# Inverse deviations of all norms: GpSimd's power instruction in place of a guess and three Newton steps on VectorE

## The reference

```
layernorm(x) = (x - mean) / sqrt(var + 1e-5)          over the 512 features of a token
layer 0: autocorrelation attention, 8 bit linear layer
layer 1: grouped attention (32 heads, 8 kv heads, biased), gated experts of rank 16
layer 2: group-wise multiplicative attention, whose result passes a group norm
         (y - mu) * rsqrt(var + 1e-5) over 16 channels x 512,
         then a permuted block-diagonal ffn with GELU
layer 3: grouped attention with rotary positions and a causal mask, SwiGLU ffn with NF4 weights
```

## Time and profile before

| | |
|---|---|
| median of 3 runs | 2106.98 us (2104.03 to 2108.8) |
| the profiled execution | 2104.66 us |
| its span in the trace | 2102.5 us |
| instructions in the trace | 26370 |
| mean granted clock of TensorE | 0.919 of full speed |
| busy, PE / PEld / DVE / ACT / POOL | 1799.7 / 1465.7 / 1516.9 / 1070.9 / 1038.0 us |

### The profile page before, as it was taken

How to read it: one execution, slowest core, us unless ns; L and a number is a source line. 1 busy time by engine, 2 the same in 40 slices (tenths; PEclk the granted TensorE clock), 3 DMA queues, 4 the chain that set the end, 5 groups by cost and what they waited for, 6 DMA issues and landing times.

```text
span 2102.5 us, 26370 instructions
## 1 busy us (share of the span) xinstructions
PE 1799.7 (86%) x8645; PEld 1465.7 (70%) x8645; DVE 1516.9 (72%) x2735; ACT 1070.9 (51%) x2556; POOL 1038.0 (49%) x889
## 2 busy tenths in 40 slices
PE   5665689999999999757677689999999999778879
PEld 3444477788888888645454478888888888657757
DVE  6666589999999985468543678888888888747740
ACT  2432467877877875431233255555555643335630
POOL 3555265555555555432133166776776742016620
PEclk7887799999999999878777899999999999889989
DMA  3002011111112111210001111111111110111120
GB/s 115 6 1 77 26 57 50 46 56 61 46 56 61 46 51 31 66 43 1 0 1 60 36 39 48 36 46 41 36 51 36 36 51 1 42 30 51 38 69 35
DMA packets 54135, 88.06 MB, mean 42 GB/s; under 512 B 9008, under 2 KB 15792, under 8 KB 53744
## 3 DMA queue, kind: packets, MB, share of 16 engines
q1 hardware_dynamic: 54000, 86.39, 13.1%
HBM read 75.62 MB, written 10.75 MB: 41 GB/s over the span
## 4 chain that ended last, share of the span: by engine, by line
PE 25%; DVE 22%; issue 19%; POOLq 13%; POOL 8%; ACT 7%; DVEq 5%; DMA 1%; SPq 0%; ACTq 0%
POOLq L326 8%; DVE b_st_u L253 6%; POOLq L324 5%; PE c_ps L66 4%; PE a_ps L66 4%; PE e_ps L66 3%; DVEq L254 3%; PE b_ps_o L66 3%; POOL d_roped L1026 3%; PE d_ps_job L66 2%; PE b_ps_job L66 2%; PE d_ps_o L66 2%; ACT b_st_sign L234 1%; POOL d_wo L1031 1%; POOL d_pt_sign L323 1%
## 5 line engine op out<-in xcount | busy, mean ns | idle before, releaser
L66 PE MATMUL b_ps_o<-b_wo,b_oT 128*128 128x512 f32 x768 | 190.0, 397 | 18.1 <-DVE b_oT L1273 18.1
L66 PE MATMUL d_ps_o<-d_wo,d_oT 128*128 128x512 f32 x768 | 190.7, 397 | 9.9 <-DVE d_oT L1272 9.7
L1026 POOL TENSOR_TENSOR d_roped<-d_rot_a,d_rot_b 128x512 f32<-128x512 f32 x80 | 104.6, 1307 | 183.6 <-DVE d_rot_b L1282 183.6
L66 PE MATMUL d_ps_job<-xnT,d_wq 128*128 128x512 f32 x768 | 193.1, 404 | 2.3 <-DVE d_rot_b L1282 2.3
L66 PE MATMUL b_ps_job<-xnT,b_wq 128*128 128x512 f32 x768 | 189.5, 400 | 5.0 <-DVE b_qT L1273 4.9
L323 POOL TENSOR_SCALAR b_pt_sign<-b_pt_sign 128x512 f32<-128x512 f32 x112 | 79.5, 710 | 222.0 <-ACT b_pt_sign L315 211.6
L66 PEld LDWEIGHTS b_ps_o<-b_wo,b_oT 128*128 128x128 f32 x768 | 145.2, 191 | 54.4 <-DVE b_oT L1273 24.4
L253 DVE SCALAR_TENSOR_TENSOR b_st_u<-b_st_sign,b_st_u 128x512 f32<-128x512 bf16 x182 | 176.2, 968 | 9.1 <-issue 0.4
L66 PEld LDWEIGHTS d_ps_o<-d_wo,d_oT 128*128 128x128 f32 x768 | 143.2, 188 | 47.7 <-DVE d_oT L1272 15.5
L66 PEld LDWEIGHTS b_ps_job<-xnT,b_wq 128*128 128x128 f32 x768 | 142.7, 191 | 35.7 <-issue 7.1
L66 PEld LDWEIGHTS d_ps_job<-xnT,d_wq 128*128 128x128 f32 x768 | 143.1, 191 | 33.5 <-issue 3.3
(11 more groups left out here) (366 smaller groups left out, 4453.8 us busy)
## 6 DMA issues: line engine op xcount, KB each, us to landing
b_raw<-in_wq_dram SPq DMA_DIRECT2D x32, 256.0 KB, 2.6
b_raw<-in_wo_dram SPq DMA_DIRECT2D x32, 256.0 KB, 2.6
d_raw<-in_wq_dram SPq DMA_DIRECT2D x32, 256.0 KB, 2.6
d_raw<-in_wo_dram SPq DMA_DIRECT2D x32, 256.0 KB, 2.7
e_nat<-dequantized SPq DMA_DIRECT2D x30, 256.0 KB, 2.9
b_st_v<-in_quantized_dram SPq DMA_DIRECT2D x13, 256.0 KB, 2.9
dequantized<-b_st_u SPq DMA_DIRECT2D x13, 256.0 KB, 2.8
a_ctx_in<-in_ctx_dram SPq DMA_DIRECT2D x8, 256.0 KB, 5.3
```

The costliest lines, as they stand in the source:

```text
L66: i = pe.matmul(out, a, b, start=first and t == 0, stop=last and t == len(terms) - 1)
L1026: pool.tensor_tensor(roped[:, n % 2], rot_a[:], rot_b[:], ALU.add).then_inc(s_sum, 1)
```

## The change

`inverse_root` goes. VectorE ends a norm with `bn_aggr` and signals `means`. GpSimd then adds epsilon, drains, and raises the result to the power of a tile that holds -0.5 (`root`), and signals; in stage `a` GpSimd makes the shift too. In stages `c` and `e` VectorE waits for the root at a later due time, so that other work of its plan may stand in between. For the group norm VectorE still adds epsilon and GpSimd does the power alone. To free semaphores, `s_early` is merged into `s_wide` (5 transfers in place of 2 and 3), `s_rows` into `s_const` (9 in place of 4 and 5), and the two `rates` semaphores of stage `a` into one. The place of each new piece in GpSimd's and VectorE's order is in the yields. The core of the diff:

```diff
-def inverse_root(dve, y, v, t, iterations=3):
-    dve.tensor_scalar(y.bitcast(I32), v.bitcast(I32), -0.5, float(0x5F3759DF), ALU.mult, ALU.add)
-    dve.drain()
-    for _ in range(iterations):
-        dve.tensor_tensor(t, y, y, ALU.mult)
-        dve.drain()
-        dve.scalar_tensor_tensor(t, t, -0.5, v, ALU.mult, ALU.mult)
-        dve.drain()
-        dve.scalar_tensor_tensor(y, t, 1.5, y, ALU.add, ALU.mult)
-        dve.drain()
...
 class QuadNorm:
-    def rates_of_stats(self, dve):
+    def means(self, dve):
         for j in range(QUAD):
-            dve.bn_aggr(self.mv[:, j], self.stats[:, j])
-        dve.drain()
-        dve.tensor_scalar(self.var[:], self.mv[:, :, 1], EPS, None, ALU.add)
-        dve.drain()
-        inverse_root(dve, self.rstd[:], self.var[:], self.tmp[:])
+            i = dve.bn_aggr(self.mv[:, j], self.stats[:, j])
+        return i
+
+    def root(self, pool):
+        pool.tensor_scalar(self.var[:], self.mv[:, :, 1], EPS, None, ALU.add)
+        pool.drain()
+        return pool.tensor_tensor(self.rstd[:], self.var[:], self.power[:], ALU.pow)
...
         # stage a, GpSimd
+            def quad(t):
+                n = norm[t]
+                yield 0.0
+                pool.memset(n.power[:], -0.5)
+                for k, name in enumerate(("rates1", "rates2", "rates3")):
+                    yield at(QUAD * t, name) + 0.1
+                    pool.wait_ge(s_means, 2 * k + t + 1)
+                    pool.tensor_scalar(shift[t][:], n.mv[:, :, 0], -1.0, None, ALU.mult)
+                    n.root(pool)
+                    pool.drain()
+                    pool.tensor_tensor(shift[t][:], shift[t][:], n.rstd[:], ALU.mult).then_inc(s_rates, 1)
...
         # stage c, GpSimd
+                def root(step, k):
+                    yield at(t, step) + 1.0
+                    waits(pool, t, ("dve", "means", k))
+                    done(norm[t].root(pool), ("root", k))
+
                 for j in J:
                     yield at(t, "cs", j)
...
+                if t:
+                    yield at(t, "rates")
+                    before(pool, 4)
+                    pool.memset(norm[t].power[:], -0.5)
+                yield from root("rates", 0)
                 for j in J:
                     yield at(t, "ffn") - 0.5
...
+                yield from root("norm2", 1)
...
+                yield at(t, "grp") + 1.0
+                waits(pool, t, ("dve", "gvar", 0))
+                done(pool.tensor_tensor(grstd[t][:], gvar[t][:], norm[t].power[:], ALU.pow), ("groot", 0))
+                yield from root("norm3", 2)
                 for h in H:
                     yield at(t, "up", h + 1)
...
+                yield from root("norm4", 3)
...
         # stage c, VectorE
+                def rates(step, k):
+                    norm[t].statistics(dve, x[t])
+                    done(norm[t].means(dve), ("means", k))
+                    yield at(t, step) + 2.5
+                    waits(dve, t, ("pool", "root", k))
...
-                norm[t].rates(dve, x[t])
+                yield from rates("norm2", 1)
...
-                inverse_root(dve, grstd[t][:], gvar[t][:], gtmp[t][:])
+                yield at(t, "grp") + 2.0
+                waits(dve, t, ("pool", "groot", 0))
...
         # stage e, GpSimd and VectorE
+            for half in (0, 1):
+                yield (0.5, 9.0)[half]
...
+                pool.wait_ge(s_means, half + 1)
+                norm[half].root(pool).then_inc(s_root, 1)
...
-                    norm[half].rates(dve, [resid[:, HALF * half + j] for j in range(HALF)])
+                    norm[half].statistics(dve, [resid[:, HALF * half + j] for j in range(HALF)])
+                    norm[half].means(dve).then_inc(s_means, 1)
+                    yield (2.0, 10.0)[half]
+                    dve.wait_ge(s_root, half + 1)
```

More of the change, by code:

```diff
@@ L339, in __init__, with statistics @@
         self.mv = sb(name + "_mean_var", [P, QUAD, 2])
-        self.var, self.rstd, self.tmp = (sb(name + x, [P, QUAD]) for x in ("_var", "_rstd", "_tmp"))
-    def rates(self, dve, xs):
+        self.var, self.rstd, self.power = (sb(name + x, [P, QUAD]) for x in ("_var", "_rstd", "_power"))
+    def statistics(self, dve, xs):
         for j in range(QUAD):
@@ L530, in chain @@
                 done(pool.tensor_tensor(x(b), x(b), bias8[:], ALU.add), "x1b")
-            yield from in_order(*(chain(b) for b in B))
+            def quad(t):
[9 more added lines that the diff above has]
+                    pool.tensor_tensor(shift[t][:], shift[t][:], n.rstd[:], ALU.mult).then_inc(s_rates, 1)
+            yield from in_order(*(quad(t) for t in (0, 1)), *(chain(b) for b in B))
         def tensor(pe):
@@ L711, in quad, with means @@
                 n = norm[t]
[L713 to L716, removed]
+                def means():
+                    n.means(dve).then_inc(s_means, 1)
                 yield at(QUAD * t, "rates1")
@@ L727, in quad @@
                     dve.drain()
-                    rates()
+                    means()
             def chain(b):
@@ L1463, in expert_group_and_permuted_ffn @@
         hT = [a[:, :, 0].rearrange("p a (j n) -> p a j n", j=QUAD) for a in xp]
-        s_small, s_early, s_wide, s_wb, s_down, s_rows, s_const = (sem(n) for n in ("small", "early", "wide", "wb_in", "down_in", "rows", "const"))
+        s_small, s_wide, s_wb, s_down, s_const = (sem(n) for n in ("small", "wide", "wb_in", "down_in", "const"))
         s_zero, s_wm, s_high, s_split, s_pick = (sem(n) for n in ("zero", "product", "high", "split", "pick"))
@@ L1488, in expert_group_and_permuted_ffn @@
         turned_order = lambda n, m: [(n, 0), (n, 1), (n, 2), (m, 0), (n, 3), (m, 1), (m, 2), (m, 3)]
[L1489 to L1492, removed]
+        dve_s = [Steps(sem(f"dve{t}"), of("y") + [("means", 0), ("xn1", 0), ("xn1", 1)] + turned_order("xn1", "t1")[2:] + [("z", 0), ("hw", 0), ("hT", 0)]
+                       + of("x1") + [("means", 1)] + of("xn2", "p") + [("row", 0), ("grp", 0), ("gvar", 0), ("affine", 0)]
+                       + of("x2") + [("means", 2)] + turned_order("xn3", "t3") + of("pick", "yT", "x3") + [("means", 3)] + turned_order("xn4", "t4")) for t in (0, 1)]
+        pool_s = [Steps(sem(f"pool{t}"), of("cs") + [("root", 0)] + of("xb") + [("root", 1)] + [(n, j) for j in J for n in ("xs", "xc")]
+                        + [("groot", 0), ("root", 2)] + [("acts", h) for h in H] + [("root", 3)]) for t in (0, 1)]
         steps = {"pe": pe_s, "act": act_s, "dve": dve_s, "pool": pool_s}
@@ L1550, in gpsimd @@
             pool.memset(raw[:, 2], 0.0).then_inc(s_zero, 1)
+            pool.memset(norm[0].power[:], -0.5)
             def thread(t):
                 done = pool_s[t].done
+                def root(step, k):
+                    yield at(t, step) + 1.0
+                    waits(pool, t, ("dve", "means", k))
+                    done(norm[t].root(pool), ("root", k))
                 for j in J:
@@ L1825, in thread @@
                 before(dve, 4 if t else 2)
-                norm[t].rates(dve, x[t])
+                yield from rates("rates", 0)
                 for j in (0, 1):
@@ L1903, in thread @@
                 dve.drain()
-                dve.tensor_scalar(gvar[t][:], gvar[t][:], EPS, None, ALU.add)
-                dve.drain()
-                inverse_root(dve, grstd[t][:], gvar[t][:], gtmp[t][:])
+                done(dve.tensor_scalar(gvar[t][:], gvar[t][:], EPS, None, ALU.add), ("gvar", 0))
+                yield at(t, "grp") + 2.0
+                waits(dve, t, ("pool", "groot", 0))
                 dve.tensor_tensor(g_a[t][:], grp[t][:, :, 0], grstd[t][:], ALU.mult)
@@ L1919, in thread @@
                 dve.drain()
-                norm[t].rates(dve, x[t])
+                yield from rates("norm3", 2)
                 yield from turned("xn3", "t3", 0)
@@ L1935, in thread @@
                 dve.drain()
-                norm[t].rates(dve, x[t])
+                yield from rates("norm4", 3)
                 yield from turned("xn4", "t4", 0)
@@ L2001, in swiglu @@
         s_down, s_x, s_out = sem("down"), sem("x"), sem("out")
+        s_means, s_root = sem("means"), sem("root")
         TILE = 12 * 3.0
@@ L2067, in gpsimd @@
         def gpsimd(pool):
-            yield 0
+            for half in (0, 1):
+                yield (0.5, 9.0)[half]
+                if half == 0:
+                    before(pool, 4)
+                    for t in (0, 1):
+                        pool.memset(norm[t].power[:], -0.5)
+                pool.wait_ge(s_means, half + 1)
+                norm[half].root(pool).then_inc(s_root, 1)
             for n in range(pt.total):
```

48 lines of the change are left out of this document (13 added, 35 removed).

## The result

| | kernel before | changed kernel |
|---|---|---|
| median of the timed executions | 2105.51 us (4) | 2071.27 us (4) |
| profiled execution / its span | 2104.66 / 2102.5 | 2073.24 / 2071.5 |
| mean granted clock of TensorE | 0.919 | 0.931 |
| VectorE busy | 1516.9 us | 1474.0 us |
| GpSimd busy | 1038.0 us | 1065.6 us |

The ratio is 0.9844 (95% interval 0.9801 to 0.9887). In a second comparison it is 0.9857 (0.9826 to 0.9887), with a median of 2070.31. So the change gains 30 to 35 us: 33 and 30 by the two ratios, 34 and 35 by the medians, 31 between the two profiled executions. 28 were forecast, and 2079 us. One execution of the kernel before took 6034.96 us and is left out everywhere. VectorE's busy time falls by 42.9 us, more than the 31 named as the least.

What follows compares the result with a forecast made beforehand. Attention stages were taken as TensorE-bound, the short stages as chains of hand-overs with no engine full. Eight terms summed to 27.7, say 28 us, off the profiled 2104.7: 2076.7, as a median 2079; range 2066 to 2108.

Steps and rivals of the forecast that it cites:

- 1, start: Start of the first layer: first root 0.8 us quicker, query product taken by VectorE at 19.7 instead of 21.8; 2.1 us gained.
- 2, its last sequence: First layer's last sequence: VectorE's low half, which TensorE waits for, no longer stands behind a whole iteration; 2.7 us gained.
- 3, second and third norm: First layer, 205 to 221 us: the two roots end at 208.2 and 212.7, the second instead of 220.8; 7 us counted.
- 4, its tail: Tail of the first attention: VectorE makes a late unit's probabilities right after the aggregation, 6.3 us sooner; 5.0 us counted.
- 5, expert layer, first half: First half of the tokens: quicker roots, gate arithmetic free of bias additions, low half before the wait; 8 us counted.
- 6, second half: Expert layer, second half: one root gains 1.2 us, roots queued behind GpSimd's low halves lose 5.8; net -4.6.
- 7, norm 4: Fourth norm of the expert layer: 3.3 us gained in the first half, 1.2 in the second; 4.5 together.
- 8, last layer: Last layer: first norm 0.3 us, second 2.7 as TensorE's low half now precedes the wait; 3.0 together.
- The price: Time of one GpSimd power instruction, at every root: at least 0.2 us, at most 3.4, taken as 1.0.
- The slope: Ten of the places go with the power's price one to one: gain is 28 - 10 (p - 1) us.
- the dear cases: Rivals at the roots: power 2 to 3.6 us, gains 2 to 18, chance 0.13; from 4.2 us slower, chance 0.17.
- The rival of the factor 1.9: Every root 1.9 times as long on GpSimd, power 4.6 us, 2115 us in all; within the slower case, chance 0.17.

Runs made afterwards that it cites:

- again: The changed kernel run once more, unaltered, for a closer ratio and a second trace; median 2070.31 us, ratio 0.9857.
- the order alone: Changed kernel's order of work, but guess and Newton steps back on VectorE and no root on GpSimd; 2105.54 us, ratio 1.0026 to the kernel before.
- the engine alone: Changed kernel, but in expert and last layers VectorE waits for each root directly behind its aggregation; 2080.57 us, ratio 0.9902 to the kernel before.
- the third trace of before: The kernel before, unaltered, traced a third time; 2097.20 us, one execution.

## Why the prediction was right

| step | forecast | changed | again |
|---|---|---|---|
| 1, start | 2.1 | 3.3 | 3.6 |
| steady part of the first layer | - | 7.3 | 12.1 |
| 2, its last sequence (180 to 190) | 2.7 | 3.4 | 3.3 |
| 3, second and third norm (190 to 242) | 7 | 7.6 | 7.8 |
| first attention | - | -2.9 | -2.9 |
| 4, its tail (895 to 947) | 5.0 | 4.8 | 4.7 |
| 5, expert layer, first half (to 1010) | 8 | 7.9 | 7.9 |
| 6, second half (to 1113) | -4.6 | -5.2 | -5.1 |
| 7, norm 4 (to 1187) | 4.5 | 2.5 | 2.4 |
| second attention | - | -1.7 | -1.7 |
| 8, last layer | 3.0 | 3.9 | 3.8 |
| sum | 27.7 | 30.9 | 35.9 |

The eight steps alone give 28.2 us in the first trace. What the forecast lacked is two things that half cancel: the steady part, and 4.6 us that the two attention stages give back. That the eight steps add up so near to 27.7 is in part luck: in the first trace steps 1, 2, 3 and 8 came out larger by 0.6 to 1.2 us each, step 6 smaller by 0.6 and step 7 by 2.0.

- *The price* was the open term and came out at 1.04. The lower bound of 0.2 was sound: a multiplication of this shape takes exactly the 0.20 that the two row durations gave. The upper bound of 3.4 was never approached. A root with nothing beside it takes 1.54 us from aggregation to tile (974.60 to 976.14), as costed.
- *Step 1* is 1.2 us larger: the query product ran at the higher clock, six matmuls from 16.87 in 1.66 us against 2.93.
- *Step 3*: the two roots end at 194.0 and 198.4 in the changed kernel, which with the lead of 14.0 us is 208.0 and 212.4; forecast were 208.2 and 212.7.
- *Step 4*: VectorE's probabilities start at 877.15, 0.13 us after the aggregation's end, and TensorE does not wait. The sum is right, but it takes both parts: the order alone gives 0.6 from 895 to 947, the engine alone 2.1.
- *Step 5*: the gate arithmetic takes 4.13 us (956.97 to 961.10) in place of 7.08 (981.13 to 988.21), 2.95 less where 3.3 were forecast.
- *Step 6*: ScalarE's affine step comes 3.6 us later against its neighbours (2.7 forecast), the third norm's tile 7.8 (7). The mechanism, two roots behind low halves, is shown by moving them. What the second norm's root gives, 1.2 in the forecast and 2.1 here, is there by 1045 (a lead of 33.5) and gone by 1058 (31.5).
- *Step 7* is the mis-sized one, 2.5 us instead of 4.5. In the first half, from the aggregation's end to the first tile, it takes 2.77 us (1088.90 to 1091.67) in place of 6.16 (1115.14 to 1121.30), the 3.4 us that were forecast as 3.3. But TensorE's wait shrinks by 2.5 only: GpSimd's next low half, from 1091.60, now runs beside the tile, which takes 1.48 us instead of 0.55. What had held up the iteration holds up the step behind it. The lead grows by 1.8 there, and by 0.8 in the second half, where 1.2 were forecast. VectorE's and GpSimd's timelines:

```profile
1088.52 0.38 DVE L308 BATCH_NORM_AGGREGATE c_norm_mean_var<-c_norm_stats 128x2 f32<-128x6 f32 x4
1091.67 3.35 DVE L317 TENSOR_SCALAR c_xn<-resid,c_norm_mean_var,c_norm_rstd 128x512 f32<-128x512 f32 x3 [2.77 <-POOL c_norm_rstd L314]
...
1091.60 2.67 POOL L1560 TENSOR_TENSOR c_cs<-c_ctx_in,c_cs 128x512 fp32r<-128x512 f32 x2
```

- *The slope* of 10 us per us holds only near 1.0. It steepens above, so the dear cases were somewhat too kind: the gain is gone at 3.3 us, not at 3.8.
- *The rival of the factor 1.9* fell. The Trainium skill (GPSIMD Engine Reference, section 4.1, Engine selection) keeps elementwise work on VectorE; at four columns a multiplication took 0.20 us on GpSimd and 0.16 on VectorE (the row at 1032.12 above), nothing like twice, and one power took the place of ten instructions. A load of code before a first call, for which the Trainium skill (GPSIMD Engine Reference, section 2.1, Instruction dispatch) gives about 6 us, did not show: between the first add, which ends at 12.45, and the first power at 12.59 lie 0.14 us.

What stays open: why the attention stages give back some of a lead (the third trace of before loses 3.2 us there as well), and what sets the pattern of the clock in the first layer.

## What to carry to other kernels

A chain of tiny instructions on a busy engine is worth moving to an idle one even at a higher price each, if the receiving engine's queue is empty at that moment. Cost the queue place, not only the instruction: two roots queued behind low halves gave back 5 us. Moving the wait of a step later gains only together with the engine that works in the meantime. And before a gain is put down to a mechanism, take a second and third trace of the kernel before: one of them was 11 us shorter in the first layer without any change.

## What the runs showed of the hardware

- GpSimd's power on 128x4 values takes 1.04 us where its multiplication takes 0.20.
- Two executions of the same kernel on one core differ by 8 us (2097.20 and 2105.05; 42 of before lie from 2092.3 to 2108.8). In their traces the difference arises in one stretch of some 150 us in which TensorE is busy about two thirds of the time, at a granted clock of 0.90 in one and 0.81 in the other.
- VectorE's normalizing step on 512 columns, 0.53 us at the least, has a median of 0.91 in the changed kernel's stage `c` and 0.55 in the kernel before. Beside GpSimd's low halves from 1091.60 two such steps took 1.48 and 1.49, though the two engines work on different tiles, and the next one, after them, 0.54.
